# Where the two operands of a matmul lie, modulo 128 bytes, in a transformer block of fp32r matmuls

## The chip, the core and the metric

One core of a Trainium2 chip runs the whole kernel. The metric is the device time of one execution in microseconds; lower is better.

## What is computed

The reference is one transformer block on x of 32 x 256 x 256 with a context of 32 x 256 x 192: self attention, cross attention and a gated feed forward, each behind a layer norm and with a residual. There are 16 heads of 64, and the feed forward is 1024 wide.

```
def _attention(xq, xkv, wq, wk, wv, wo, bo):
    q = (xq @ wq).reshape(B, S, N_HEADS, D_HEAD)      # k, v alike from xkv
    attn = jnp.einsum('bihd,bjhd->bhij', q, k) * D_HEAD ** (-0.5)
    attn = jax.nn.softmax(attn, axis=-1)
    out = jnp.einsum('bhij,bjhd->bihd', attn, v).reshape(B, S, D_ATTN)
    return out @ wo + bo

h = _layernorm(x, ln1_g, ln1_b)
x = _attention(h, h, sa_wq, sa_wk, sa_wv, sa_wo, sa_bo) + x
h = _layernorm(x, ln2_g, ln2_b)
x = _attention(h, cond_emb, ca_wq, ca_wk, ca_wv, ca_wo, ca_bo) + x
h = _layernorm(x, ln3_g, ln3_b)
p = h @ ff_w1 + ff_b1
a, gate = (p[..., :D_FF], p[..., D_FF:])
return a * jax.nn.gelu(gate, approximate=False) @ ff_w2 + ff_b2 + x
```

## The kernel before

The kernel is written engine by engine: each engine has its own instruction list, and semaphores order them. Three stages follow each other: 32 passes of self attention, 32 of cross attention (64 passes in all, one batch each, software pipelined), and 32 iterations of the feed forward.

Every fp32 value that goes into a matmul is split into a high and a low part (`x_hi`, `x_lo`, both fp32r), and a product is the three matmuls high x high, high x low, low x high (`three` and `product`, L593). ACT writes the high part by a copy, DVE or POOL the low part by a subtraction. `nc.tensor.matmul(dst, a, b)` loads `a` into the array (a weight load, PEld) and streams `b` past it (PE). The profile's rows name the operands the other way round, streamed before loaded: `unit_ps<-w_hi,a_hi` streams `w_hi` and loads `a_hi`. One load and one matmul belong together, the load of the next runs beside the matmul before it.

A pass of attention has four steps. In each, PE does in order: `scores` of two head pairs (L606, 24 matmuls of 64 rows, in pairs for the left and the right half of the partitions), then the units of the step (`STEP_UNITS`: two q and k projections of 12 matmuls each, "v" of 6 with 512 columns, or "wo", the output projection of 24), then `attend` (L618, 16 matmuls). In the cross attention the output projection of the last step is cut in two, and its first 12 matmuls (`project_out(..., 0)`) stand straight behind the scores.

The feed forward runs over m = 0 to 7: `hidden(t, m)` is 12 matmuls into `s_ps` (value and gate), and `down(t, m - 2)` 6 matmuls into `unit_ps`, behind it. Between them ACT does the gelu and `a_hi`, DVE the gating, POOL `a_lo`. The first iteration (START) begins inside `end_attention`: PE does transposes, output half 0 of the last batch, attend, `hidden` of m = 0 to 2, attend, `hidden` of m = 3, output half 1, and then goes on with m = 4. The feed forward's three weights (two of `ff_w1` and `ff_w2`) are loaded into `w_stage` slots 0, 1 and 2 during the cross attention and split by `split_ff_weight` at the turn, while PE works.

| matmuls | loaded | streamed | before | changed |
|---|---|---|---|---|
| q and k projections, `hidden` | weights | `hT` | 0 / 64 | 0 / 64 |
| values ("v") | `hT` | weight | 64 / 0 | 64 / 0 |
| `scores` | queries | keys | 64 / 64 | 0 / 64 |
| `attend` | `v_f` | `pT` | 64 / 0 | 64 / 0 |
| output ("wo"), `down` | `a` | weight | 64 / 0 | 0 / 64 |

Of the kernel before, what the change touches and what calls it, by code (L numbers as in the profile page):

```python
# [10 lines left out]
P = 128  # L11
# [142 lines left out]
def columns_of(w, piece, slot):  # L154

    _, cols = columns(piece)
    if cols is None:
        return w[:, slot, piece[1] * DA:(piece[1] + 1) * DA]
    return w[:, slot, :].rearrange("p (k n) -> p k n", k=DK)[:, :, cols]

def block_kernel(nc, x, ctx, ln1_g, ln1_b, ln2_g, ln2_b, ln3_g, ln3_b, sa_wq, sa_wk, sa_wv, sa_wo, sa_bo,
# [4 lines left out]
    with stack:  # L167
# [50 lines left out]
        qk_hi = sb("qk_hi", [P, RING, 2, S], F32R)  # L218
        qk_lo = sb("qk_lo", [P, RING, 2, S], F32R)
# [213 lines left out]

        def tiles(a):
            return a.rearrange("(i p) d -> p i d", p=P)
# [12 lines left out]
        def _(sp):  # L448
# [15 lines left out]
            def load_cross_weight(slot, quarter):  # L464
# [4 lines left out]
                if w.shape[0] == DFF:  # L469
                    rows = PAIRS // 4  # L470
                    sp.dma_start(w_stage[:, slot, cols].rearrange("p (k n) -> p k n", k=rows),
# [3 lines left out]
                if w.shape[0] == DC and k:  # L475
                    sp.dma_start(w_stage[LEFT, slot, cols], w[P:, part]).then_inc(ca_ld, 16)
                    sp.dma_start(w_stage[RIGHT, slot, cols], w[P:, part]).then_inc(ca_ld, 16)
                else:
                    sp.dma_start(w_stage[:, slot, cols], w[k * P:(k + 1) * P, part]).then_inc(ca_ld, 16)

            def load_ff_weight(k, quarter):
# [3 lines left out]
                if len(w.shape) == 3:  # L485
                    rows = w.shape[1] // 4
                    sp.dma_start(w_stage[:, k, cols].rearrange("p (k n) -> p k n", k=rows),
                                 w[:, quarter * rows:(quarter + 1) * rows, :]).then_inc(ff_ld[k], 16)
                else:
                    sp.dma_start(w_stage[:, k, cols], w[:, cols]).then_inc(ff_ld[k], 16)  # L490
# [95 lines left out]
        def _(pe):  # L586
# [35 lines left out]
            def projection(slot, cols, side, tokens):  # L622

                terms = []
                for k in range(DK):
                    w = slice(k * DA + cols.start, k * DA + cols.stop)
                    if side == 1 and k == DK - 1:
                        terms += [(w_hi[:, slot, w], hT_hi[:, side, k, tokens]), (w_lo[:, slot, w], hT_hi[:, side, k, tokens])]
                    else:
                        terms += three(w_hi[:, slot, w], w_lo[:, slot, w], hT_hi[:, side, k, tokens], hT_lo[:, side, k, tokens])  # L630
                return terms

            def project_out(t, home, unit, it):
# [4 lines left out]
                if it == 0:  # L638
                    at.bank_free(pe, t, unit)
                    if isinstance(b, int) and b == ph.first:  # L640
# [5 lines left out]
                                for term in three(a_hi[:, m, rows], a_lo[:, m, rows], w_hi[:, 3, m * D:(m + 1) * D],  # L646
                                                  w_lo[:, 3, m * D:(m + 1) * D])])
# [696 lines left out]
```

## Time and profile before

| | |
|---|---|
| three runs, median | 2865.21 us (2864.95 to 2866.52) |
| the profiled execution: its time, its span | 2866.0 us, 2864.2 us |
| PE busy | 2842.0 us (99%), 25278 matmuls |
| DVE, ACT, POOL busy | 2256.3 (79%), 1912.3 (67%), 1471.1 us (51%) |
| granted clock of TensorE | 0.998 on average, 1.00 in the long stretches |

The profile is of one execution. Start times are records; the ends of matmuls are modelled and overlap, so how fast PE goes is read from the distance between starts or from a count of matmuls in a stretch, not from the mean duration of one. The self attention ends near 1180 us, the cross attention near 2306, the rest is the feed forward.

### The profile page before, as it was taken

Reading aid. Unit: us, or ns where it says so; the run is one execution under the profiler, and the core shown is the slowest. Engines: PE = TensorE matmul, PEld = TensorE weight load, DVE = VectorE, ACT = ScalarE, POOL = GpSimd, SP = SyncE. Lnnn points to the kernel's source line nnn. Section 1 sums busy time; section 2 is a strip of 40 time slices with the busy share of each in tenths; the row PEclk is TensorE's granted clock in tenths of the full one; section 3 lists DMA queues with packets and bytes.
Section 4 is the critical chain, followed back from the end, with each engine's and each line's share of the span. In section 5 each row is a group of like instructions: output and inputs, shape, how many; then the busy total and the mean of one; then the engine's idle time right before and its main releaser. Section 6 shows DMA issues by size and latency. Waiting matters only on the chain.

```text
span 2864.2 us, 72446 instructions
## 1 busy us (share of the span) xinstructions
PE 2842.0 (99%) x25278; PEld 2485.3 (87%) x25278; DVE 2256.3 (79%) x3495; ACT 1912.3 (67%) x6041; POOL 1471.1 (51%) x1310
## 2 busy tenths in 40 slices
PE   8999999999999999999999999999999999999999
PEld 6888888888888888888888888888888889999999
DVE  6888888888888888888888888888888865555554
ACT  6677766677766776777777777777777754444443
POOL 5444444444444444765555555555555544554554
PEclk9999999999999999999999999999999999999999
DMA  5666666666666666667777776666766632222222
GB/s 147 158 162 157 156 157 159 158 154 145 151 151 154 150 148 149 161 166 177 177 172 169 173 171 169 168 164 165 168 168 163 151 100 88 73 73 84 81 73 63
DMA packets 355360, 413.32 MB, mean 144 GB/s; under 512 B 122048, under 2 KB 209472, under 8 KB 355264
## 3 DMA queue, kind: packets, MB, share of 16 engines
q1 hardware_dynamic: 345120, 395.29, 57.4%
q10 hardware_dynamic: 10144, 16.78, 1.6%
q8 instruction: 56, 0.92, 0.1%
q14 instruction: 40, 0.33, 0.0%
HBM read 94.52 MB, written 49.02 MB: 50 GB/s over the span
## 4 chain that ended last, share of the span: by engine, by line
PE 98%; DVE 1%; ACT 1%; POOL 0%; issue 0%; DMA 0%; DVEq 0%; POOLq 0%; ACTq 0%
PE unit_ps L593 54%; PE o_ps L618 17%; PE s_ps L606 14%; PE s_ps L593 12%; DVE neg_max L1021 0%; ACT probs L851 0%; DVE blocks L1035 0%; POOL probs L1253 0%; DMA x_ln<-in_x_dram 0%; ACT qk_hi L882 0%; DVE qk_lo L1046 0%; DVE hT L1016 0%; DVE hT_lo L1059 0%; ACT x_n L828 0%; ACT L828 0%
## 5 line engine op out<-in xcount | busy, mean ns | idle before, releaser
L1253 POOL TENSOR_TENSOR probs<-probs,row_inv 128x1024 f32<-128x1024 f32 x512 | 967.8, 1896 | 893.9 <-DVE row_inv L1026 893.9
L851 ACT ACTIVATE probs<-s_ps,neg_max 128x256 f32<-128x256 f32 x2048 | 950.4, 487 | 403.9 <-DVE neg_max L1021 403.4
L1021 DVE TENSOR_REDUCE neg_max<-s_ps 128x4 f32<-128x1024 f32 x512 | 616.8, 1205 | 62.8 <-PE s_ps L606 58.4
L1035 DVE STREAM_TRANSPOSE blocks<-probs 128x1024 f32<-128x1024 f32 x512 | 633.2, 1237 | 19.9 <-POOL probs L1253 19.9
L593 PE MATMUL unit_ps<-hT_hi,w_hi 128*128 128x256 f32 x2048 | 571.3, 282 | 3.0 <-DVE hT_lo L1059 2.6
L593 PE MATMUL unit_ps<-hT_hi,w_lo 128*128 128x256 f32 x2048 | 554.0, 277 | 0.0
L618 PE MATMUL o_ps<-pT,v_f 128*64 128x256 f32 x4096 | 498.5, 385 | 1.7 <-DVE a_lo L1041 1.7
L593 PE MATMUL unit_ps<-hT_lo,w_hi 128*128 128x256 f32 x1792 | 496.1, 277 | 0.0
L851 ACT ACTIVATION_READ_ACCUMULATOR probs<-s_ps,neg_max 128x1 f32 x2048 | 444.6, 217 | 0.0
L593 PE MATMUL unit_ps<-w_hi,a_hi 128*128 128x256 f32 x1536 | 430.8, 280 | 3.8 <-DVE a_lo L1041 2.8
L593 PE MATMUL unit_ps<-w_lo,a_hi 128*128 128x256 f32 x1536 | 425.7, 277 | 0.0
L593 PE MATMUL unit_ps<-w_hi,a_lo 128*128 128x256 f32 x1536 | 425.7, 277 | 0.0
L618 PEld LDWEIGHTS o_ps<-pT,v_f 128*64 128x64 f32 x4096 | 271.7, 136 | 174.6 <-issue 48.0
L1046 DVE TENSOR_TENSOR qk_lo<-unit_ps,qk_hi 128x512 fp32r<-128x512 f32 x512 | 350.8, 685 | 76.8 <-ACT qk_hi L882 62.5
L593 PEld LDWEIGHTS unit_ps<-hT_hi,w_hi 128*128 128x128 f32 x2048 | 384.3, 188 | 21.2 <-issue 1.5
L593 PEld LDWEIGHTS unit_ps<-hT_hi,w_lo 128*128 128x128 f32 x2048 | 384.6, 188 | 0.0
L593 PEld LDWEIGHTS unit_ps<-hT_lo,w_hi 128*128 128x128 f32 x1792 | 336.8, 188 | 5.7
L1268 POOL TENSOR_TENSOR a_lo<-probs,a_hi 128x256 fp32r<-128x256 f32 x256 | 188.3, 741 | 264.9 <-ACT a_hi L900 263.0
L895 ACT ACTIVATE probs<-s_ps,b_col 128x256 f32<-128x256 f32 x256 | 121.7, 476 | 300.2 <-PE s_ps L593 300.2
L606 PE MATMUL s_ps<-qk_hi 64*128 64x256 f32 x2048 | 315.2, 304 | 6.0 <-DVE qk_lo L1046 6.0
L882 ACT CAST qk_hi<-unit_ps 128x512 fp32r<-128x512 f32 x512 | 313.9, 613 | 6.4 <-PE unit_ps L593 4.6
L1080 DVE SCALAR_TENSOR_TENSOR probs<-s_ps,b_col,probs 128x256 f32<-128x256 f32 x256 | 123.4, 482 | 240.7 <-ACT probs L895 238.7
(73 smaller groups left out, 6017.8 us busy)
## 6 DMA issues: line engine op xcount, KB each, us to landing
pT<-blocks SPq DMA_DIRECT2D x1024, 256.0 KB, 4.5
rows_t_dram<-row_blocks SPq DMA_DIRECT2D x91, 256.0 KB, 4.4
rows_in<-rows_t_dram SPq DMA_DIRECT2D x91, 256.0 KB, 4.1
x_res<-in_x_dram SPq DMA_DIRECT2D x32, 256.0 KB, 4.1
x_sa_dram<-x_out SPq DMA_DIRECT2D x32, 256.0 KB, 4.3
x_ln<-x_sa_dram ACTq DMA_DIRECT2D x32, 256.0 KB, 4.9
ctx_in<-in_ctx_dram SPq DMA_DIRECT2D x32, 256.0 KB, 4.4
x_res<-x_sa_dram SPq DMA_DIRECT2D x32, 256.0 KB, 4.1
```

What stands on the lines that cost most here:

```text
L593: last = nc.tensor.matmul(dst, a, b, start=start and n == 0, stop=stop and n == len(terms) - 1)
L606: last = nc.tensor.matmul(s_ps[:, m % 2, hd, it * S:(it + 1) * S], q[part, r, 0, rows], k[part, r, 1, :], start=n == 0, stop=n == 2)
L618: last = nc.tensor.matmul(o_ps[part, i, :], v_f[:, jt, 2 * (2 * n + i) + hd, :], p[:, jt, hd], start=jt == 0, stop=jt == IT - 1)
L851: op = nc.scalar.activation(probs[:, m % 2, r, :].rearrange("p (j b c) -> p j b c", j=IT, c=BLK), scored.rearrange("p (j c b) -> p j b c", ...
L882: nc.scalar.copy(qk_hi[:, unit[1] % RING, :, :], bank.rearrange("p (a s) -> p a s", a=2)).then_inc(at.qk_hi, 1)
L895: nc.scalar.activation(gate[:, m % 2, :], s_ps[:, m % 4 // 2, m % 2, S:2 * S], ACT.Gelu, bias=b1_col[:, FT + m:FT + m + 1]).then_inc(ff.ga ...
L1021: nc.vector.tensor_reduce(neg_max[:, m % RING, :], s_ps[:, m % 2, :, :].rearrange("p h (i j) -> p (h i) j", j=S), AX_X, ALU.max, negate=Tr ...
L1035: nc.vector.transpose(blocks[:, n % 2, :, m % 2, :].rearrange("p b (j r c) -> p r j b c", j=IT, c=BLK), probs[:, m % 2, :, :].rearrange("p ...
L1046: nc.vector.tensor_tensor(qk_lo[:, m % RING, :, :], unit_ps[:, bank_of(("qk", m)), :].rearrange("p (a s) -> p a s", a=2), f32(qk_hi[:, m % ...
L1080: nc.vector.scalar_tensor_tensor(hid[:, m % 2, :], s_ps[:, m % 4 // 2, m % 2, 0:S], b1_col[:, m:m + 1], gate[:, m % 2, :], ALU.add, ALU.mu ...
L1253: nc.gpsimd.tensor_tensor(probs[:, m % 2, :, :], probs[:, m % 2, :, :], row_inv[:, m % RING, :].unsqueeze(2).broadcast_to([P, ROWS, S]), A ...
L1268: nc.gpsimd.tensor_tensor(a_lo[:, m, :], hid[:, m % 2, :], f32(a_hi[:, m, :]), ALU.subtract).then_inc(ff.u_lo, 1)
```

## The change

The slots 0 to 2 of the weights now form `w_hi_loaded` and `w_lo_loaded`; slot 3, the one that is streamed by output and `down`, becomes a tensor of its own behind 16 floats, so at 64 modulo 128. `ff_w2` goes into slot 3 and no longer into slot 2. Since slot 3 holds the output weight until the last output projection, its split waits for that, half by half. The fillers around `a_hi` and `a_lo` are gone, which puts them at 0. Queries and keys of a head pair get a gap of 16 floats, so the keys lie 1088 bytes behind their queries and not 1024, and a filler ahead puts the queries at 0.

```
-        w_hi = sb("w_hi", [P, 4, WCOLS], F32R)
-        w_lo = sb("w_lo", [P, 4, WCOLS], F32R)
-        w_stage = sb("w_stage", [P, STAGES, WCOLS])
+        def weights(name):
+            loaded = sb(f"{name}_loaded", [P, 3, WCOLS], F32R)
+            sb(f"{name}_between", [P, 16])
+            streamed = sb(f"{name}_streamed", [P, WCOLS], F32R)
+            sb(f"{name}_behind", [P, 16])
+            return [loaded[:, i, :] for i in range(3)] + [streamed[:]]
+
+        w_hi, w_lo = weights("w_hi"), weights("w_lo")
+        w_raw = sb("w_raw", [P, STAGES, WCOLS])
+        w_stage = [w_raw[:, i, :] for i in range(STAGES)]
...
-        qk_hi = sb("qk_hi", [P, RING, 2, S], F32R)
-        qk_lo = sb("qk_lo", [P, RING, 2, S], F32R)
+        sb("before_queries", [P, 16])
+        qk_hi = sb("qk_hi", [P, RING, 2, S + 16], F32R)[:, :, :, 0:S]
+        qk_lo = sb("qk_lo", [P, RING, 2, S + 16], F32R)[:, :, :, 0:S]
+        sb("behind_queries", [P, 16])
...
-        sb("before_attended", [P, 16])
         a_hi = sb("a_hi", [P, PAIRS, S], F32R)
         a_lo = sb("a_lo", [P, PAIRS, S], F32R)
-        sb("behind_attended", [P, 16])
...
@@ down (PE)
                     last = product(bank[:, 0:D], three(a_hi[:, m, rows], a_lo[:, m, rows],
-                                                       w_hi[:, 2, m * D:(m + 1) * D], w_lo[:, 2, m * D:(m + 1) * D]),
+                                                       w_hi[3][:, m * D:(m + 1) * D], w_lo[3][:, m * D:(m + 1) * D]),
...
@@ iteration of the feed forward (PE)
                         for d in {4: (0,), 5: (1,), 6: (2, 3), 7: (4, 5)}.get(m, ()) if parts == START else ...
+                            if d == FT // 2 and parts == START:
+                                pe.wait_ge(ff_w2_lo, 2)
                             down(t, d)
...
@@ ACT
+            def split_down_weight(half):
+                act.wait_ge(at.wo_full, 2 * TOTAL - 1 + half)
+                if half == 0:
+                    act.wait_ge(ff_ld[2], 16 * 4)
+                cols = down_half(half)
+                nc.scalar.activation(w_hi[3][:, cols], w_stage[2][:, cols], ACT.Copy).then_inc(ff_hi_done, 1)
...
-                split_ff_weight(2)
+                split_down_weight(0)
...
@@ iteration of the feed forward (ACT; POOL has the same two lines, after its residual)
+                    if m == BEGUN and parts == START:
+                        split_down_weight(1)
...
@@ POOL
+            def split_down_weight(half):
+                pool.wait_ge(ff_hi_done, 3 + half)
+                cols = down_half(half)
+                nc.gpsimd.tensor_tensor(w_lo[3][:, cols], w_stage[2][:, cols], f32(w_hi[3][:, cols]), ALU.subtract).then_inc(ff_w2_lo, 1)
```

The order of PE's instructions stays as it was. In the last iterations of the feed forward, `down` between two `hidden` reads in the kernel before:

```order
L593 MATMUL s_ps<-hT_hi,w_lo 128x256
L593 MATMUL unit_ps<-w_hi,a_hi 128x256 [waits ff_u_lo]
L593 MATMUL unit_ps<-w_lo,a_hi 128x256
L593 MATMUL unit_ps<-w_hi,a_lo 128x256
L593 MATMUL unit_ps<-w_hi,a_hi 128x256
L593 MATMUL unit_ps<-w_lo,a_hi 128x256
L593 MATMUL unit_ps<-w_hi,a_lo 128x256
L593 MATMUL s_ps<-hT_hi,w_hi 128x256 [waits ff_hid_done]
```

and in the changed one:

```order
L603 MATMUL s_ps<-hT_hi,w_lo_loaded 128x256
L603 MATMUL unit_ps<-w_hi_streamed,a_hi 128x256 [waits ff_u_lo]
L603 MATMUL unit_ps<-w_lo_streamed,a_hi 128x256
L603 MATMUL unit_ps<-w_hi_streamed,a_lo 128x256
L603 MATMUL unit_ps<-w_hi_streamed,a_hi 128x256
L603 MATMUL unit_ps<-w_lo_streamed,a_hi 128x256
L603 MATMUL unit_ps<-w_hi_streamed,a_lo 128x256
L603 MATMUL s_ps<-hT_hi,w_hi_loaded 128x256 [waits ff_hid_done]
```

Only the tensors have changed. On ACT, at the turn from attention to feed forward, the kernel before has (the first row is the split of slot 1, `a_hi<-o_ps` are the evacuations of attend, `b_col` marks the gelu):

```order
L805 ACTIVATE w_hi<-w_stage 128x2048 [waits ff_ld1]
L904 CAST hT_hi<-hT 128x512 [waits ff_h_done,at_v_full]
L805 ACTIVATE w_hi<-w_stage 128x2048 [waits ff_ld2]
L861 CAST a_hi<-o_ps 128x512 [waits at_wo_full,at_o_full]
```

and the changed one, with the rows around m = 4 behind it:

```order
L817 ACTIVATE w_hi_loaded<-w_raw 128x2048 [waits ff_ld1]
L923 CAST hT_hi<-hT 128x512 [waits ff_h_done,at_v_full]
L824 ACTIVATE w_hi_streamed<-w_raw 128x1024 [waits ff_ld2,at_wo_full]
L880 CAST a_hi<-o_ps 128x512 [waits at_wo_full,at_o_full]
...
L919 CAST a_hi<-probs 128x256 [waits ff_hid_done]
L824 ACTIVATE w_hi_streamed<-w_raw 128x1024 [waits at_wo_full]
L914 ACTIVATE probs<-s_ps,b_col 128x256 [waits ff_hid_done,ff_p_full]
```

The split of the down weight has become two halves, each with a wait on an output projection. On POOL the same place in the changed kernel reads (before, the first row was one of 128x2048 and the second, `L1294`, was not there):

```order
L1294 TENSOR_TENSOR w_lo_streamed<-w_raw,w_hi_streamed 128x1024 [waits ff_hi_done]
L1289 TENSOR_TENSOR a_lo<-probs,a_hi 128x256 [waits ff_u_hi]
...
L1289 TENSOR_TENSOR a_lo<-probs,a_hi 128x256 [waits ff_u_hi] x3
L1261 TENSOR_TENSOR x_rb<-x_res,out_bias 128x512 [waits ff_res_ld]
L1294 TENSOR_TENSOR w_lo_streamed<-w_raw,w_hi_streamed 128x1024 [waits ff_hi_done]
L1289 TENSOR_TENSOR a_lo<-probs,a_hi 128x256 [waits ff_u_hi] x4
```

The second half stands behind the residual `x_rb` and ahead of the `a_lo` of m = 4.

## Rows read from the trace of the kernel before

**Rows 1.** The page, whole run: busy time of the engines; chain by engine.
```profile
PE 2842.0 (99%) x25278; PEld 2485.3 (87%) x25278; DVE 2256.3 (79%) x3495; ACT 1912.3 (67%) x6041; POOL 1471.1 (51%) x1310
...
PE 98%; DVE 1%; ACT 1%; POOL 0%; issue 0%; DMA 0%; DVEq 0%; POOLq 0%; ACTq 0%
```

**Rows 2.** Table by stretches: self attention and feed forward (columns: stretch, length, then by engine).
```profile
300.00:1150.00 850.00, 850.00 (x7599) 719.57 (x7600) 702.49 (x1019) 597.90 (x1968) 407.66 (x301) 1.00 0.65 153
...
2350.00:2850.00 500.00, 500.00 (x4309) 500.00 (x4308) 275.50 (x593) 206.50 (x510) 249.67 (x385) 1.00 0.26 77
```

**Rows 3.** Timeline (start us, us, engine, line): last key remainder, first load of scores.
```profile
1830.28 0.69 DVE L1046 TENSOR_TENSOR qk_lo<-unit_ps,qk_hi 128x512 fp32r<-128x512 f32 x1 [0.30 <-ACT qk_hi L882]
...
1831.18 0.19 PEld L606 LDWEIGHTS s_ps<-qk_hi 64*128 64x128 f32 x2 [0.38 <-DVE qk_lo L1046]
```

**Rows 4.** Timeline of PE, feed forward: starts of two successive m and a third.
```profile
2342.09 0.28 PE L593 MATMUL s_ps<-hT_hi,w_hi 128*128 128x256 f32 x1
...
2344.22 0.28 PE L593 MATMUL s_ps<-hT_hi,w_hi 128*128 128x256 f32 x1
...
2344.57 0.28 PE L593 MATMUL s_ps<-hT_hi,w_hi 128*128 128x256 f32 x1
...
2346.27 0.28 PE L593 MATMUL s_ps<-hT_hi,w_hi 128*128 128x256 f32 x1
```

**Rows 5.** Timeline of PE, self attention: projection behind scores, then output.
```profile
508.15 0.28 PE L593 MATMUL unit_ps<-hT_lo,w_hi 128*128 128x256 f32 x1
...
508.50 0.28 PE L593 MATMUL unit_ps<-hT_lo,w_hi 128*128 128x256 f32 x1
...
513.38 0.28 PE L593 MATMUL unit_ps<-w_hi,a_lo 128*128 128x256 f32 x1
```

**Rows 6.** Timeline of PE: two stretches of hidden, each behind an attend.
```profile
2319.66 0.28 PE L593 MATMUL s_ps<-hT_hi,w_hi 128*128 128x256 f32 x1
...
2323.29 0.28 PE L593 MATMUL s_ps<-hT_hi,w_lo 128*128 128x256 f32 x1
...
2325.60 0.28 PE L593 MATMUL s_ps<-hT_lo,w_hi 128*128 128x256 f32 x1
...
2326.77 0.28 PE L593 MATMUL s_ps<-hT_hi,w_lo 128*128 128x256 f32 x1
```

**Rows 7.** Timeline of PE, batch 29 of the feed forward: down of m = 2, then m = 3.
```profile
2813.75 0.28 PE L593 MATMUL unit_ps<-w_hi,a_hi 128*128 128x256 f32 x1
...
2814.45 0.28 PE L593 MATMUL s_ps<-hT_hi,w_hi 128*128 128x256 f32 x1
...
2816.51 0.28 PE L593 MATMUL s_ps<-hT_hi,w_hi 128*128 128x256 f32 x1
```

**Rows 8.** Timeline of PE, cross attention: output behind scores, then a projection.
```profile
1501.39 0.28 PE L593 MATMUL unit_ps<-w_lo,a_hi 128*128 128x256 f32 x1
...
1502.68 0.28 PE L593 MATMUL unit_ps<-hT_hi,w_hi 128*128 128x256 f32 x1
...
1503.04 0.28 PE L593 MATMUL unit_ps<-hT_hi,w_hi 128*128 128x256 f32 x1
```

**Rows 9.** Timeline of PE: pairs of score matmuls, the second and the last of twelve.
```profile
506.53 0.28 PE L606 MATMUL s_ps<-qk_lo,qk_hi 64*128 64x256 f32 x2
...
507.72 0.28 PE L606 MATMUL s_ps<-qk_hi,qk_lo 64*128 64x256 f32 x2
```

**Rows 10.** Groups by shape, whole run: busy us, mean ns of one.
```profile
L1268 POOL TENSOR_TENSOR a_lo<-probs,a_hi 128x256 fp32r<-128x256 f32 x256 | 188.3, 741 | 264.9 <-ACT a_hi L900 263.0
...
L1248 POOL TENSOR_TENSOR w_lo<-w_stage,w_hi 128x1024 fp32r<-128x1024 f32 x8 | 19.2, 2403 | 2.3 <-ACT w_hi L799 1.4 <-DVE hT_lo L1063 0.9
...
L799 ACT ACTIVATE w_hi<-w_stage 128x1024 fp32r<-128x1024 f32 x8 | 8.8, 1094 | 0.5 <-ACT x_n L828 0.5
```

**Rows 11.** Timeline at the start of the feed forward: residual; first matmul of down of m = 4.
```profile
2332.97 1.28 POOL L1240 TENSOR_TENSOR x_rb<-x_res,out_bias 128x512 f32<-128x512 f32 x1
...
2338.62 0.28 PE L593 MATMUL unit_ps<-w_hi,a_hi 128*128 128x256 f32 x1
```

More of the change, by code:

```diff
@@ L432, in straight, with down_half @@
             return rows.rearrange("p (k j c) -> p k j c", c=BLK, j=NB)
+        def down_half(half):
+            return slice(half * WCOLS // 2, (half + 1) * WCOLS // 2)
         def tiles(a):
@@ L470, in load_cross_weight @@
                     rows = PAIRS // 4
-                    sp.dma_start(w_stage[:, slot, cols].rearrange("p (k n) -> p k n", k=rows),
+                    sp.dma_start(w_stage[slot][:, cols].rearrange("p (k n) -> p k n", k=rows),
                                  w.rearrange("(k p) n -> p k n", p=P)[:, quarter * rows:(quarter + 1) * rows, :]).then_inc(ca_ld, 16)
@@ L475, in load_cross_weight @@
                 if w.shape[0] == DC and k:
[L476 to L477 removed]
+                    sp.dma_start(w_stage[slot][LEFT, cols], w[P:, part]).then_inc(ca_ld, 16)
+                    sp.dma_start(w_stage[slot][RIGHT, cols], w[P:, part]).then_inc(ca_ld, 16)
                 else:
[L479 removed]
+                    sp.dma_start(w_stage[slot][:, cols], w[k * P:(k + 1) * P, part]).then_inc(ca_ld, 16)
             def load_ff_weight(k, quarter):
@@ L486, in load_ff_weight @@
                     rows = w.shape[1] // 4
-                    sp.dma_start(w_stage[:, k, cols].rearrange("p (k n) -> p k n", k=rows),
+                    sp.dma_start(w_stage[k][:, cols].rearrange("p (k n) -> p k n", k=rows),
                                  w[:, quarter * rows:(quarter + 1) * rows, :]).then_inc(ff_ld[k], 16)
                 else:
-                    sp.dma_start(w_stage[:, k, cols], w[:, cols]).then_inc(ff_ld[k], 16)
+                    sp.dma_start(w_stage[k][:, cols], w[:, cols]).then_inc(ff_ld[k], 16)
             def in_register(value):
@@ L627, in projection @@
                     if side == 1 and k == DK - 1:
-                        terms += [(w_hi[:, slot, w], hT_hi[:, side, k, tokens]), (w_lo[:, slot, w], hT_hi[:, side, k, tokens])]
+                        terms += [(w_hi[slot][:, w], hT_hi[:, side, k, tokens]), (w_lo[slot][:, w], hT_hi[:, side, k, tokens])]
                     else:
-                        terms += three(w_hi[:, slot, w], w_lo[:, slot, w], hT_hi[:, side, k, tokens], hT_lo[:, side, k, tokens])
+                        terms += three(w_hi[slot][:, w], w_lo[slot][:, w], hT_hi[:, side, k, tokens], hT_lo[:, side, k, tokens])
                 return terms
@@ L645, in project_out @@
                                [term for m in range(half * HALF, (half + 1) * HALF)
-                                for term in three(a_hi[:, m, rows], a_lo[:, m, rows], w_hi[:, 3, m * D:(m + 1) * D],
-                                                  w_lo[:, 3, m * D:(m + 1) * D])])
+                                for term in three(a_hi[:, m, rows], a_lo[:, m, rows], w_hi[3][:, m * D:(m + 1) * D],
+                                                  w_lo[3][:, m * D:(m + 1) * D])])
                 if it == IT - 1:
@@ L694, in hidden @@
                     last = product(s_ps[:, m % 4 // 2, m % 2, half * S:(half + 1) * S],
-                                   [term for k in range(DK) for term in three(w_hi[:, k, cols], w_lo[:, k, cols],
+                                   [term for k in range(DK) for term in three(w_hi[k][:, cols], w_lo[k][:, cols],
                                                                               hT_hi[:, parity, k, :], hT_lo[:, parity, k, :])])
@@ L1299, in iteration @@
                         deviation(ff, t + 2)
+                    if m == BEGUN and parts == START:
+                        split_down_weight(1)
                     if "cur" in parts:
```

11 lines of the change are left out of this document (5 added, 6 removed).

## The prediction

> **What bounds the kernel now.** I read the page first, then the table by stretches, the chain of waits, and last the timeline of PE alone, because the first three say that only its finest grain is left. The page gives PE 99% of the span and the chain that ended last lies on PE for 98% of it [rows 1]. In the stretches by time PE has no idle time at the full granted clock of 1.00, while DVE is busy for 83% (702.49 of 850.00 us) and 55% (275.50 of 500.00), ACT and POOL for less [rows 2]. No other engine is close, and the one that feeds the scores is early: the key remainder is written at 1830.28 + 0.69 = 1830.97 and the scores' first weight load comes at 1831.18 [rows 3]. So the time is the sum over PE's matmuls of the distance from one start to the next; the ends in the profile are modelled, the starts are records. Only a change of that spacing, or of the stalls between kinds of work, moves the total.
>
> **Two spacings.** In the feed forward 4309 matmuls take 500 us, 116.0 ns each [rows 2]. The timeline shows that this is a mean of two values. One m (12 matmuls of `hidden`, 6 of `down`) goes from 2342.09 to 2344.22, 118.3 ns each, the next from 2344.22 to 2346.27, 113.9 ns [rows 4]; their mean, 116.1, is that of the 500 us, so they alternate through the whole feed forward. The instructions are the same in both. In the attention, 43 spacings of a projection and the output from 508.50 to 513.38 take 4.88 us, 113.5 ns each [rows 5]. I call 113.4 (the 32 spacings of [rows 6] in 3.63 us) the short spacing and 118 the long one.
>
> What decides between them? Sorted by the places of the two operands, the rows say this. (a) `hidden` and the q, k projections have the loaded operand at 0 and the streamed one at 64; `down` and the output have 64 and 0. (b) A `down` at the short spacing is followed by a `hidden` at the long one, which keeps it and hands it to its `down`; the next `hidden` needs 0.35 us for three spacings and is short from then on [rows 4]. (c) It is not m's parity. The long m that starts at 2342.09 is m = 1, all odd ones are like it, and in batch 29, m = 2 starts short, but its `down` takes 0.70 us for six, 117 ns, from 2813.75 to 2814.45, after a single matmul that came a few ns late. The next m, 3, is then short, 2.06 us to 2816.51 [rows 7], and odd and even have changed places up to the end. So the spacing is a state that the stream carries along, and the change of kind at the end of `down` switches it. (d) An output block straight behind scores (in the cross attention) runs at the long spacing, 1501.39 to 1502.68 for 11 spacings, and the projection behind it needs 0.36 us for three and then is short [rows 8]. A projection straight behind scores needs 0.35 us for its first three spacings, 508.15 to 508.50, and is short from there [rows 5]. (e) Scores, 64 against 64, have ten spacings of pairs in 1.19 us, 119 ns [rows 9].
>
> **The change, term by term.** It puts all of output, `down`, `hidden`, projections and scores at loaded 0 and streamed 64. Values (loaded 64, streamed 0) and attend stay.
>
> 1. Feed forward. The switch between kinds at the end of each `down` is gone. If the stream stays at 113.4, it gains 116.0 - 113.4 = 2.6 ns on each of 4608 matmuls (32 batches x 8 m x 18, by the code): 12.2 us. Bounds: nothing (116.0 stays), and all at 118, which costs (118 - 116.0) x 4608 = +9.2 us. I take the gain, because (a) to (d) put the loss at the switch and a uniform stretch of both kinds has held the short spacing for 43 in a row.
> 2. Scores. 64 x 4 steps x 10 spacings = 2560. The trace has no scores at 0 and 64. The nearest rows are single matmuls at those places, 113.4, and today's 119. I take 117, since a pair is two loads and two matmuls and each start has its own spacing in the unit, and since the first three after a start are longer anywhere: -2.0 x 2560 = -5.1 us. Bounds: 113.4 gives -14.3; the long spacing carried over (119 + 2.7) gives +6.9 us.
> 3. Output behind scores, in 32 passes of the cross attention: 11 x (117.3 - 113.4) + 3 x (120 - 116) = 55 ns each, -1.7 us; bounds 0 and -2.0.
> 4. The turn. The down weight now lies where the output weight lay, so its split into high and low part waits for the output projection, in two halves. One copy of 128x2048 on ACT becomes two of 128x1024 (1.09 us each), one subtraction on POOL becomes two of 2.40 us [rows 10]. The first half waits on ACT for output half 0 of the last batch; behind it on ACT stands only the evacuation of the attend that PE begins after that output and that takes longer than 1.09 us (16 matmuls, 8 pairs of over 0.2 us). The second stands on ACT before the gelu of m = 4 and is released when the output ends. PE then still has the 12 matmuls of `hidden` of m = 4 before it, 1.4 us, so the copy of 1.09 us is hidden with 0.3 us to spare. On POOL it stands behind the residual that ends at 2332.97 + 1.28 = 2334.25 and delays `a_lo` of m = 4 to 2336.65 + 0.74 = 2337.4 (0.74 is the 741 ns of one in [rows 10]); PE wants it, and the weight of the new wait, at 2338.62 [rows 11]. That is 1.2 us to spare, and `gated` of m = 6 on DVE, which waits for the same `a_lo`, has its gelu behind it and not PE. I put this at nothing; without that cover it would be 1 to 2 us, once.
> 5. A gap of 64 bytes between queries and keys makes the writes of `qk_hi` and `qk_lo` two runs of 256 instead of one of 512. The trace has no such pair of shapes to compare; the same elements are moved, so I take nothing, and even a tenth of 0.69 us would leave 0.14 of the 0.21 us before the scores' load [rows 3].
>
> The sum is -12.2 - 5.1 - 1.7 = -19.0 us. The profiled execution took 2866.0 us (its span 2864.2), which makes 2847.0; the median of the three runs, 2865.21, is 0.8 below it, so the sum gives 2846.2 there. I say 2847.0.
>
> **A rule against the change.** The stretches of [rows 4] are equal instructions at 118.3 and 113.9 ns, so loading and streaming do disturb each other here. The Trainium skill, TensorE: Matmul & The Clock Gate, "Step-by-step: what each phase is for", says otherwise: TensorE has two independent read ports, and loading the next weights takes no bandwidth from the running matmul. SBUF — State Buffer, "Who interferes with whom", adds that PE never waits on anyone. By that rule the places of the operands are nothing and terms 1 to 3 are zero; by the rows they are -19.0.
>
> **The rivals.**
> - *Places don't matter (the loss hangs on something else that alternates, such as the destination bank).* For it: the forecast rests on correlation in one trace. Against: (c), since the banks kept their order when the spacings changed places. Time 2865.2. Chance 0.06.
> - *The long spacing is kept.* This one ends on the other side. In a uniform stream nothing switches, so nothing lifts the stream out either. For it: a `hidden` that starts behind attend, already at 0 and 64, takes 1.17 us for the ten spacings from 2325.60 to 2326.77, 117 ns, and does not recover [rows 6], and every recovery of the feed forward is at a switch. Against: the other start of that kind is short from its fourth matmul, as are all behind scores and values. If the feed forward sits at 118, the terms give +9.2 - 5.1 - 1.7 = +2.4 us, 2867.6 (chance 0.09); if the scores keep it too, +9.2 + 6.9 - 1.7 = +14.4, 2879.6 (chance 0.04). It decides from the point where 57% of the feed forward's matmuls are long (2.6 / 4.6), where term 1 is zero.
> - *Scores alone get slower*, the loads of two halves meeting the streams in a worse way: -12.2 - 1.7 + 6.9 = -7.0, 2858.2. Chance 0.12.
> - *The feed forward gains only in part*, long after each start or small delay until something lifts it: half of term 1, 2852. Chance 0.04.
> - The forecast: 0.65. Its own range is 2842 to 2853.
>
> **How the numbers follow.** The lower end, 2838, takes nearly the whole bound of term 2 (2865.2 - 12.2 - 14.3 - 1.7 = 2837.0). The upper end, 2861, takes in scores that get slower and the partial gain; left out are the first two rivals, 0.19. The three runs of before lie within 1.6 us, and 0.2% (5.7 us) is about what a measurement can tell from no change. Faster than 2859.5: forecast, scores alone, part of the gain, 0.81, less 0.02 for the edges of those ranges; slower than 2870.9: 0.04 and a share of the milder case of the second rival, 0.07; the rest, 0.14, is within.
>
> **What the profile of the changed kernel would show.** Term 1: 18 matmuls of each m in 2.04 us, no alternation, and 4410 matmuls in 500 us. Term 2: ten spacings of score pairs in 1.17 us. Term 3: the output block behind scores at 113 to 114 ns. Term 4: no idle time of PE between 2320 and 2345. The forecast is wrong if the feed forward still has two spacings, or one at 118, or if the scores' pairs stand at 120 and more.

## The result: 2875.5 us, slower by 0.31%

The changed kernel takes 2875.53 us (median of 8 runs, 2873.01 to 2876.85), the kernel before beside it 2866.31 us (8 runs). The ratio is 1.0031, 95% interval 1.0020 to 1.0042. The prediction said 2847.0 us, and its range ended at 2861.

The page of the changed kernel (busy time, then the chain that ended last) answers to [rows 1]:

```profile
PE 2851.5 (99%) x25278; PEld 2491.1 (87%) x25278; DVE 2258.2 (79%) x3495; ACT 1909.2 (66%) x6042; POOL 1469.6 (51%) x1311
...
PE 98%; DVE 1%; ACT 0%; POOL 0%; issue 0%; DMA 0%; DVEq 0%; POOLq 0%; ACTq 0%
```

PE is still the bound, with as many matmuls, and is busy 9.5 us longer. The table by stretches answers to [rows 2]:

```profile
300.00:1150.00 850.00, 850.00 (x7543) 718.74 (x7542) 698.19 (x1013) 592.77 (x1954) 403.54 (x299) 1.00 0.65 152
2350.00:2850.00 500.00, 500.00 (x4356) 500.00 (x4355) 279.97 (x604) 207.74 (x514) 254.51 (x393) 1.00 0.26 78
```

In 850 us of self attention PE now starts 7543 matmuls and not 7599; in 500 us of feed forward 4356 and not 4309, 114.8 ns each and not 116.0. So the feed forward gained and the attention lost. Measured from the first score matmul of a pass to that of the next, in the timeline of PE:

- a pass of self attention 36.97 us, before 36.71: +0.267 x 31 = +8.3 us;
- a pass of cross attention 35.07 us, before 34.91: +0.160 x 31 = +5.0 us;
- an m of the feed forward 2.067 us, before 2.127 and 2.053 in turn, mean 2.090: -0.023 x 248 = -5.7 us;
- the turn: from the last score matmul to the end it is 558.7 us, before 560.4; with the feed forward's -5.7 taken out, +3.9 us.

The last score matmul starts 12.4 us later than before (the two lines on the passes give 13.3, since the first and last pass of each kind are incomplete). 12.4 - 5.7 + 3.9 = +10.6; the spans, 2874.9 and 2864.2, differ by 10.7.

**Feed forward.** Timeline of PE, starts of `hidden`, `down` and the next `hidden`:

```profile
2601.94 0.28 PE L603 MATMUL s_ps<-hT_hi,w_hi_loaded 128*128 128x256 f32 x1
...
2603.30 0.28 PE L603 MATMUL unit_ps<-w_hi_streamed,a_hi 128*128 128x256 f32 x1
...
2604.00 0.28 PE L603 MATMUL s_ps<-hT_hi,w_hi_loaded 128*128 128x256 f32 x1
```

Twelve matmuls of `hidden` take 1.36 us, 113.3 ns each, in nearly every m (241 of 253): the alternation of [rows 4] is gone. But six of `down` take 0.70 us, 117 ns. **Output** in self attention, from its first matmul to the attend behind it:

```profile
402.23 0.28 PE L603 MATMUL unit_ps<-w_hi_streamed,a_hi 128*128 128x256 f32 x1
...
405.14 0.44 PE L628 MATMUL o_ps<-pT,v_f 128*64 128x256 f32 x2
```

It takes 2.91 us for 24; the block of before took 2.81, at the short spacing of [rows 5]. That is 91 ns, twice a pass, 5.6 us over 31 passes. Both are the kinds that the change moved from 64/0 to 0/64 modulo 128.

**The turn.** The waits of PE between 2300 and 2345 us (engine, line, waited for: us in total, times, longest), then the timeline there:

```profile
PE s_ps L603 <- DVE hT_lo L1115: 3.2, 1, 3.2
```

```profile
2330.53 2.90 DVE L1115 TENSOR_TENSOR hT_lo<-hT,hT_hi 128x512 fp32r<-128x512 f32 x1
...
2330.16 2.72 POOL L1294 TENSOR_TENSOR w_lo_streamed<-w_raw,w_hi_streamed 128x1024 fp32r<-128x1024 f32 x1 [5.47 <-ACT w_hi_streamed L824]
```

The first `hidden` waits 3.2 us for `hT_lo`, which takes 2.90 us and ends 0.55 us behind POOL's half of the down weight's subtraction. The profile of before has no wait for `hT_lo` there.

### The profile page after: what moved, and what is told of

It reads as the page before. It is cut to its first block, busy times and chain, and to the rows that moved or that the text cites. A ratio compares the mean times of both kernels' runs of the same rounds, so it can differ in the third digit from the quotient of the medians.

```text
span 2874.9 us, 72450 instructions
## 1 busy us (share of the span) xinstructions
PE 2851.5 (99%) x25278; PEld 2491.1 (87%) x25278; DVE 2258.2 (79%) x3495; ACT 1909.2 (66%) x6042; POOL 1469.6 (51%) x1311
## 4 chain that ended last, share of the span: by engine, by line
PE 98%; DVE 1%; ACT 0%; POOL 0%; issue 0%; DMA 0%; DVEq 0%; POOLq 0%; ACTq 0%
PE unit_ps L603 55%; PE o_ps L628 16%; PE s_ps L616 14%; PE s_ps L603 12%; DVE neg_max L1042 0%; DVE blocks L1056 0%; ACT probs L870 0%; POOL probs L1274 0%; DMA x_ln<-in_x_dram 0%; ACT qk_hi L901 0%; DVE w_lo_loaded L1008 0%; PE unit_ps L768 0%; DVE hT_lo L1115 0%; DVE qk_lo L1067 0%; DVE hT L1037 0%
## 5 line engine op out<-in xcount | busy, mean ns | idle before, releaser
L603 PE MATMUL unit_ps<-hT_hi,w_hi_loaded 128*128 128x256 f32 x2048 | 572.7, 283 | 1.9 <-DVE hT_lo L1080 1.5
L603 PE MATMUL unit_ps<-hT_hi,w_lo_loaded 128*128 128x256 f32 x2048 | 556.2, 278 | 0.0
L603 PE MATMUL unit_ps<-hT_lo,w_hi_loaded 128*128 128x256 f32 x1792 | 497.3, 278 | 0.0
L603 PE MATMUL unit_ps<-w_hi_streamed,a_hi 128*128 128x256 f32 x1536 | 433.4, 282 | 3.8 <-DVE a_lo L1062 2.8
L603 PE MATMUL unit_ps<-w_hi_streamed,a_lo 128*128 128x256 f32 x1536 | 429.8, 280 | 0.0
L603 PE MATMUL unit_ps<-w_lo_streamed,a_hi 128*128 128x256 f32 x1536 | 429.8, 280 | 0.0
L603 PEld LDWEIGHTS unit_ps<-hT_hi,w_hi_loaded 128*128 128x128 f32 x2048 | 384.8, 188 | 20.9 <-issue 1.6
L603 PEld LDWEIGHTS unit_ps<-hT_hi,w_lo_loaded 128*128 128x128 f32 x2048 | 384.9, 188 | 0.0
L603 PEld LDWEIGHTS unit_ps<-hT_lo,w_hi_loaded 128*128 128x128 f32 x1792 | 337.5, 188 | 6.0
```

The lines of the kernel that those rows point to most:

```text
L603: last = nc.tensor.matmul(dst, a, b, start=start and n == 0, stop=stop and n == len(terms) - 1)
```

## The experiments

Five kernels named micro leave the whole block out and run only TensorE's stream. The others compute everything. The excerpts of code are shortened to the lines that matter. A place is a byte address modulo 256, of which 0, 64, 128 and 192 occur. The kernel before has the weights at 128 and `hT`, `a`, queries and keys at 64. In the changed kernel the loaded weights lie at 128 (high part) and 0 (low part), the streamed ones at 192 and 64, `a` at 128, queries and keys at 128 and 192 or at 0 and 64 by slot. The text on the change speaks only of modulo 128. `v_f` and `pT` also move by 128 in the changed kernel; micro3 has a configuration with these two moved alone, and its passes stay within 2 ns, so they are left aside.

**micro1: a map of places**

```python
for s in range(PLACES):
    for l in range(PLACES):
        apart()                       # one matmul on 64 rows
        for i in range(24):
            matmul(ps[:, 0, 0:256], at(loaded, l, i % 2, 128), at(streamed, s, i % 2, 256))
```

> A kernel with nothing but matmuls; the whole block is left out. For each of 16 places of the loaded and 16 of the streamed operand, 64 bytes apart and taken modulo 1024, it issues 24 matmuls of 256 columns with all 128 rows, then pairs on two halves of 64 rows, then for 4 by 4 places matmuls of 512 columns. Theory A (the prediction's): what counts is the place modulo 128, so the 16 by 16 table of the mean spacing is a checkerboard of four kinds that repeats every two places, with 113.4 ns at loaded 0 and streamed 64 and about 118 at others. Theory B: a larger period counts, 256 or more, so that the output of the changed kernel (loaded 128, streamed 64 or 192 modulo 256) reads 118 in the table and the kernel before (loaded 64, streamed 128) reads 113.4. Theory C: places count for nothing, and all 256 cells are within 1 ns of one another.

The mean of the last 12 spacings in each stretch, worked out from the starts, repeats every 256 bytes and in nothing smaller (one cell takes either 118.4 or 120.0):

```
ns per matmul      loaded 0   64     128    192
streamed   0       120.0     113.3   118.4  117.8
          64       113.3     120.0   117.8  118.8
         128       118-120   117.8   120.0  113.3
         192       113.3     119.0   113.3  120.0
```

The rows of the timeline show it without any working. They are the single matmuls ahead of (loaded 0, streamed 64), ahead of (64, 64) and behind that:

```profile
71.78 0.32 PE L51 MATMUL ps<-streamed,loaded 64*128 64x128 f32 x1
...
74.95 0.32 PE L51 MATMUL ps<-streamed,loaded 64*128 64x128 f32 x1
...
78.26 0.32 PE L51 MATMUL ps<-streamed,loaded 64*128 64x128 f32 x1
```

3.17 us for the one and 3.31 for the other, with the same instructions. Theory A falls: loaded 0 and streamed 64 modulo 128 is four cells of this table, three at 113.3 and one, (128, 64), at 117.8, and that one is the low weight's place under output and `down` of the change. Pairs of matmuls on 64 rows, in the mean of the ten spacings behind the first, do best, 57.0 to 57.5 ns per matmul, where the loaded operand is 64 bytes behind the streamed one modulo 256; at 64 and 64, as before, they take 59.0 to 59.6, and 64 bytes ahead, as in the change, 58.9 or 59.0.

**micro2: the kernel's own order, TensorE alone**

```python
for c in CONFIGS:                     # places of weights, hT, a, queries, keys
    for unit in "SvpvOSpwOSvpvOSpwO" + "hd" * 9:
        part(c, unit)                 # scores, values, projections, attend, output, hidden, down
```

> TensorE's stream of the kernel by itself (one self-attention pass and nine m of the feed forward, in the kernel's order, with its hi and lo terms), for many places of the operands in SBUF; no other engine works and the rest of the block is left out. Theory B (places modulo 256 bytes decide, the table of micro1): with the places of the kernel before, one pass takes about as long per block as in its profile and the m of the feed forward take 2.05 to 2.13 us; with those of the change the output blocks take about 90 ns more and each m about 2.07 us, though no other engine works; and with weights at 0, hT at 64 and a at 64 modulo 256 each m takes 18 x 113.3 = 2.04 us and an output block of 24 takes 2.72 to 2.80 us. Theory D (other engines' traffic in SBUF disturbs the loads): the differences between the places of before and of the change are gone when TensorE is alone.

With the places of before, m takes 2.127 and 2.053 us in turn, as in the kernel; with those of the change 2.067, and its output block 2.905. No other engine runs, so theory D falls for these two: the places of TensorE's own operands are enough. Two forecasts were wrong. With weights at 0, `hT` and `a` at 64, m takes 2.072 and 2.108 us and the output block 2.823. And the self-attention pass hardly differed, 36.89 us with the places of before and 36.88 with those of the change, where the profiles have 36.71 and 36.97; micro4 finds why.

**w0, gap, turn: one piece at a time**

```diff
 w0:    +        sb("before_weights", [P, 32])
          w_hi = sb("w_hi", [P, 4, WCOLS], F32R)
          w_lo = sb("w_lo", [P, 4, WCOLS], F32R)
        +        sb("behind_weights", [P, 32])
 gap:   +        sb("before_queries", [P, 16])
        +        qk_hi = sb("qk_hi", [P, RING, 2, S + 16], F32R)[:, :, :, 0:S]      (qk_lo too)
 turn:  down reads slot 3; split_ff_weight(2) becomes split_down_weight(0) and (1), as in the change
```

> The kernel before with one edit: the weights begin 128 bytes later, at 0 modulo 256 in place of 128; everything else keeps its place modulo 256 bytes, and nothing changes its place modulo 128. Theory A (places modulo 128, the prediction's): no change, ratio 1.000. Theory B (places modulo 256, micro1): hidden and projections (loaded 0, streamed 64) and down and output (loaded 64, streamed 0) stand at 113.3 ns from a cold start, so each m of the feed forward takes 2.04 us and not 2.05 and 2.13 in turn: 12 us less, 1 to 2 us less from output behind scores, and 0 to 4 us more from values, where micro1 has 232.7 ns for 64 and 0 and 229.8 for 64 and 128: 2852 to 2857 us, ratio 0.995 to 0.997. Theory C (only the state of the stream counts): feed forward alternates as before.

2896.51 us, ratio 1.0113 (1.0096 to 1.0130). Nothing was moved modulo 128, so places modulo 128 can't be the rule. My own forecast from micro1 had the wrong sign. The timeline shows a projection behind scores, first matmul to the first of the output behind it:

```profile
399.54 0.39 PE L595 MATMUL unit_ps<-hT_hi,w_hi 128*128 128x256 f32 x1
...
402.48 0.28 PE L595 MATMUL unit_ps<-w_hi,a_hi 128*128 128x256 f32 x1
```

2.94 us, with 118 ns from start to end, at places (loaded 0, streamed 64) that micro1 ran at 113.3. The same places can hold either spacing; which one depends on how the stretch begins, here behind scores. The kernel before shows the same from the other side: the projection of [rows 5] loads at 128 and streams at 64, 117.8 in the map, and runs at the short spacing. micro2 has 2.936 us for this block in its place in the order, and 2.072 and 2.108 us for m; w0 has 2.931 and the same 2.072 and 2.108. A self pass is 0.453 us longer and a cross pass 0.533, the feed forward the same in the mean: 31 x 0.986 = +30.6 us. So the map of places is not enough; places and order together told this block and m.

> The kernel before with the queries and keys part of the change alone: queries at 128 or 0 modulo 256 and keys 1088 bytes behind. The prediction's term 2 gives -5.1 us. micro1's pairs give 58.9 ns per matmul for these places and 59.4 for those of before, so theory B expects 6144 x 0.5 = -3 us, less what the first projections behind scores lose (about 0.07 us a pass in the changed kernel, if the scores' places are its cause: +4). So between -3 and +1 us by theory B, with the scores' own ten spacings at 118.

2874.11 us, ratio 1.0031 (1.0018 to 1.0043): the scores' part of the change costs as much alone as the whole change, and my range of -3 to +1 us was wrong. The scores themselves gain, about 45 ns a pass of self attention and 22 of cross attention. What stands behind them loses in the cross attention: a projection behind scores 2.698 us and not 2.612, the output behind it 2.922 and not 2.814, though their own places are those of before: what the scores leave behind decides. A cross pass is 0.33 us longer, a self pass 0.08 shorter, in sum 7.6 us.

> The kernel before with the turn of the change alone: the down weight in slot 3, split behind the output projection in two halves, every place modulo 256 as before. The prediction's term 4: nothing. Rival (shared SBUF port of VectorE and GpSimd): GpSimd's first half, 2.4 to 2.7 us, starts before VectorE's hT_lo of the first feed forward batch and holds it from 0.69 to about 2.9 us; TensorE waits about 3 us there, and the total is 3 us longer, ratio 1.001.

2866.23 us, ratio 1.0003 (0.9993 to 1.0013). The turn alone costs nothing in the median, and in the profiled execution the collision doesn't happen. (The ten times reach from 2863.84 to 2869.35 us, three of them above 2868; whether it happens in those is not shown.) Timeline:

```profile
2318.30 0.69 DVE L1108 TENSOR_TENSOR hT_lo<-hT,hT_hi 128x512 fp32r<-128x512 f32 x1
...
2318.85 2.39 POOL L1287 TENSOR_TENSOR w_lo<-w_stage,w_hi 128x1024 fp32r<-128x1024 f32 x1 [6.39 <-ACT w_hi L817]
```

Here DVE comes first, by 0.55 us. In the changed kernel POOL came first, by 0.37. The clock differs between the two. The output whose end releases the first half runs at the granted clock of 0.50, 1.2 GHz, in this kernel (and in the one before), after a wait of 2.8 us for `a_lo`; in the changed kernel, after an equal wait, it runs at 1.00. The table by stretches, for turn and then for the changed kernel (the third number from the end is the granted clock):

```profile
2313.30:2315.80 2.50, 2.50 (x12) 2.50 (x13) 2.50 (x3) 0.76 (x1) 0.00 (x0) 0.50 1.06 265
```

```profile
2325.50:2328.40 2.90, 2.90 (x24) 2.82 (x24) 2.90 (x4) 0.80 (x1) 0.00 (x0) 1.00 1.03 251
2333.60:2336.60 3.00, 3.00 (x17) 3.00 (x18) 1.69 (x4) 0.71 (x1) 0.00 (x0) 0.63 0.00 0
```

So in the changed kernel the output ends 1.4 us earlier against DVE's work, POOL's half starts 0.9 us earlier, and the slow clock comes after the new wait instead. Why the clock fell at another point after the same wait is not settled. The new turn is not what keeps it up: gap, keys_first and best have the turn of before, their clock stayed at 1.00 there, and then PE waits for `hT_lo` in them too, 1.0 us. Waits of PE in gap between 2290 and 2355 us:

```profile
PE s_ps L595 <- DVE hT_lo L1096: 1.0, 1, 1.0
```

So about 2.2 of the 3.2 us belong to the longer `hT_lo`, the rest to an execution at full clock.

**turn_apart: the changed kernel without the collision**

```diff
                 residual(at, TOTAL - 1, ca.norm)
+                pool.wait_ge(ff.x_lo, 1)
                 split_down_weight(0)
```

> The changed kernel with one wait more: GpSimd's first half of the down weight's subtraction starts only when VectorE has written the first feed forward batch's hT_lo. Theory (the two shared a port): hT_lo takes 0.69 us and not 2.90, TensorE waits about 1 us and not 3.2 us between the last attend but one and the feed forward, and the total is 2 to 3.3 us less than the changed kernel's 2875.5, so about 2872.7, ratio to before 1.0025. Rival (hT_lo was long for another reason, or the wait only moves): 2875.5 as before it, ratio 1.003.

2872.06 us, ratio to before 1.0024 (1.0013 to 1.0035); its span, 2871.2, is 3.7 below that of the changed kernel, and the passes are the same. Of the 3.7, 2.2 are the shorter wait and most of the rest the slow clock behind it, which this execution doesn't have. Against the kernel before beside each, the medians differ by 7.0 us here and by 9.2 in the changed kernel; the two intervals of the ratio overlap. `hT_lo` is back at 0.68 us and the wait at 1.0:

```profile
2330.56 0.68 DVE L1115 TENSOR_TENSOR hT_lo<-hT,hT_hi 128x512 fp32r<-128x512 f32 x1
```

The collision is shown: the same instruction takes 2.90 us beside POOL's and 0.68 without it. The Trainium skill, SBUF — State Buffer, "Who interferes with whom", has it as a rule: a VectorE instruction with two SBUF inputs contends with a GpSimd instruction that reads SBUF. By that rule the trace agrees (0.68 and 2.90 us). The prediction never looked for it.

**micro3, micro4, micro5: how far the stream alone tells the time**

```diff
 micro3: high and low parts at places of their own; the cross-attention pass added
 micro4: slots of queries and keys 2048 bytes apart (micro2, micro3: shifted by 128 in every second slot)
 micro5: the places of change and after256, then 120 placements
```

> TensorE's stream alone again (a self-attention half pass twice, a cross-attention pass, six m of the feed forward), with high and low parts at places of their own and queries and keys apart from each other; the rest of the block is left out. Theory E (phase: the places modulo 256 bytes and the phase in which a stretch begins decide together, as micro2 suggests, since w0 and micro2 agree): with the places of each kernel already timed, the stream alone takes the time of its profile within 20 ns a pass: self-attention pass 36.71 us for before, 36.97 for the change, 36.63 for the gap alone; cross-attention pass 34.91, 35.07 and 35.23; m 2.127 and 2.053, 2.067, 2.127 and 2.053. Rival (other engines' accesses take part): the sums differ from these profiles by more than 0.1 us a pass. The sweep of the other places says whether some placement lies below all of them: theory E allows one, with no forecast of where.

For the change 36.972 and 35.091 us, for the gap alone 36.626 and 35.229, as expected, with 24 ns too much in one pass. For before 36.893 and 35.028, and the profile has 36.707 and 34.907. That looked like the rival, until I saw that my stream shifted every second slot of the queries by 128 bytes, which before doesn't.

> The stream alone, with the slots of queries and keys 2048 bytes apart, as in the kernel before (micro2 and micro3 had shifted every second slot by 128 bytes, as the change does). Theory E, the stream alone decides: with the places of the kernel before, the self-attention pass is now 36.71 us and the cross-attention pass 34.91, as in its profile (micro3, with the shift: 36.89 and 35.03). Rival: the 0.19 and 0.12 us between micro3 and the profile come from what other engines do, and stay. The second half gives six m of the feed forward for 256 placements of the four parts of down's operands, twice; theory E gives no forecast of the best, only that 18 x 113.3 = 2.04 us is the floor.

With the slots right, the stream alone gives 36.708 and 34.906 us for the places of before. Its timeline, first score matmuls of a half pass, of the cross pass and of what follows:

```profile
123.45 0.39 PE L82 MATMUL s_ps<-qk_hi 64*128 64x256 f32 x2
...
141.81 0.38 PE L82 MATMUL s_ps<-qk_hi 64*128 64x256 f32 x2
...
176.71 0.39 PE L82 MATMUL s_ps<-qk_hi 64*128 64x256 f32 x2
```

18.36 us is half of the 36.71, and 34.90 the cross pass. The second half found seven placements of `down` with 2.040 us for each m, all with the streamed weight at 64. The plainest has `a` at 0. First `hidden` of three m:

```profile
2480.56 0.28 PE L64 MATMUL s_ps<-hT_hi,w_hi 128*128 128x256 f32 x1
...
2482.60 0.28 PE L64 MATMUL s_ps<-hT_hi,w_hi 128*128 128x256 f32 x1
...
2484.64 0.28 PE L64 MATMUL s_ps<-hT_hi,w_hi 128*128 128x256 f32 x1
```

> The stream alone: a self-attention pass, a cross-attention pass and four m of the feed forward, first for the places of the changed kernel and of after256, then for 120 placements with queries and keys at one place or 64 bytes apart, with the weights of output and down at 128 (as before) or at 64 modulo 256 with a at 0. Theory E: the first configuration repeats the changed kernel's profile (36.97, 35.07 and 2.067 us) and the following ones tell after256 in advance; the m of the feed forward is 2.04 us wherever down's operands are at loaded 0 and streamed 64 modulo 256 and hidden's at 128 and 64. Rival: a pass or an m is off by more than 0.05 us.

The change's configuration gives 36.974 and 35.091 us, that of after256 36.626 and 35.100. Of its four m the two in the middle, which the ends of the short stretch don't touch, take 2.067 us for the change and 2.040 for after256 and for every placement with `down` at 0 and 64. No other placement beats keys_first in the attention.

**keys_first, after256, best: kernels chosen by the stream alone**

```diff
 keys_first (on before):
-        qk_hi = sb("qk_hi", [P, RING, 2, S], F32R)
+        sb("before_keys", [P, 32])
+        qk_hi = sb("qk_hi", [P, RING, 2, S + 16], F32R)[:, :, :, 0:S]      (qk_lo too)
-        q[part, r, 0, rows], k[part, r, 1, :]
+        q[part, r, 1, rows], k[part, r, 0, :]
 after256 (on the change):
-            sb(f"{name}_between", [P, 16])
+            sb(f"{name}_between", [P, 48])
-        sb("behind_queries", [P, 16])
+        sb("behind_queries", [P, 48])
 ...
 best (on keys_first):
+            raw = sb(name, [P, 4 * WCOLS + 48], F32R)
+            return [raw[:, i * WCOLS:(i + 1) * WCOLS] for i in (0, 1, 3, 2)], raw[:, 3 * WCOLS + 48:4 * WCOLS + 48]
```

> The kernel before with the keys ahead of the queries: loaded queries 64 bytes behind the streamed keys modulo 256 (keys at 192 and 64, queries at 0 and 128), nothing else moved modulo 256. By the prediction's rule of places modulo 128 this is the same kind as the change's scores (0 and 64), so theory A expects what the gap alone gave, 2874. Theory E reads micro3: self-attention pass 36.61 us and cross-attention pass 34.83, against 36.71 and 34.91 before, so 31 x 0.094 + 31 x 0.080 = 5.4 us less: 2860 us, ratio 0.998. The rival that this falls: the stream falls into its slower branch by other engines' timing, and the total is 2865 or more.

2860.21 us, ratio 0.9981 (0.9972 to 0.9990), forecast 2860. (The projections also write the other half of the bank, so that one copy still moves both.) Modulo 128 its scores are the change's, loaded at 0 and streamed at 64; modulo 256 the loaded one is 64 bytes behind and not ahead. A self pass is 36.613 us and a cross pass 34.827, within 1 ns what the stream alone had.

> The changed kernel with the same 0 and 64 of output and down, made to hold modulo 256 and not only modulo 128: a at 0 (not 128), the streamed weights, high and low, both at 64 (not 192 and 64), the loaded ones both at 128. Nine small tensors share one so that it fits. Theory A (places modulo 128): nothing changes, 2875.5. Theory E: micro4 gives 2.040 us for each m in place of 2.067, 6.6 us less; the output blocks go from 2.905 us to between 2.81 and 2.92, 0 to 11 us less; so 2857 to 2869.

2860.34 us, ratio 0.9981 (0.9971 to 0.9990): the changed kernel with output and `down` held to loaded 0, streamed 64 modulo 256, 15 us faster than the change. m takes 2.040 us, and the output in self attention 2.812. The 3.1 us wait at the turn is still in it. This kernel also moves the low part of the loaded weights back, from 0 to 128, so the 15 us are not those of output and `down` alone. micro5's third configuration is the change with only their places moved: 36.814 and 34.846 us a pass, m 2.040. Against the change in the same stream that is 31 x 0.160 + 31 x 0.245 + 248 x 0.027 = 19 us, an estimate for a kernel that was not run; the low part's return gains 0.19 us more in a self pass and loses 0.25 in a cross pass.

> The kernel before with keys_first's scores and, in the feed forward alone, down's operands at loaded 0 and streamed 64 modulo 256 (its weight 192 bytes behind the values' weight, which now lies in the last slot, and a written 64 bytes lower there); output, projections and values stay where they were. Theory E adds what was read apart: 5.4 us less from the two attention passes (micro5: 36.612 and 34.827 us, against 36.708 and 34.906) and 248 x (2.090 - 2.040) = 12.4 us less from the feed forward: 2865.2 - 17.8 = 2847.4, ratio 0.9938. Rival: the two don't add, since the feed forward keeps the phase in which the attention leaves it, as the kernel before does: 2860, ratio 0.998.

2847.70 us (5 runs, 2846.39 to 2849.05), ratio 0.9943 (0.9929 to 0.9956), forecast 2847.4. The two parts add. Its feed forward in 490 us (4223 matmuls in the kernel before, in the same 490):

```profile
2350.00:2840.00 490.00, 490.00 (x4323) 489.90 (x4321) 272.67 (x587) 206.18 (x511) 247.85 (x383) 1.00 0.26 78
```

## Why the prediction was wrong

**The step that failed** is (a) in "Two spacings": "`hidden` and the q, k projections have the loaded operand at 0 and the streamed one at 64; `down` and the output have 64 and 0", with places taken modulo 128. The trace of before cannot tell 0 from 128. Of the pairs that the change made under output and `down`, 128 with 192 occurs in no row of it, and 128 with 64 occurs only as that of `hidden` and the projections, which [rows 4] show at both spacings. Shown by w0 (nothing moves modulo 128, +31 us), by micro1's table, and by after256, which makes the same kind hold modulo 256 and gains 15 us, with micro5's third configuration.

**Term 1** (-12.2) was half right. That a uniform feed forward stays at 113.3 holds for `hidden`, and where the places suit, for all 18: 2.040 us in after256 and best, the forecast's number. In the change `down` stays at 117 to 118, and the term is -5.7. It lay within the term's own bounds.

**What had no term** was the rest of the attention. The prediction moved output and priced only its blocks straight behind scores; values and projections it took as unmoved, but modulo 256 their low weight goes from 128 to 0. A self pass is longer by 182 ns in output (91, twice), 72 in values and 53 in projections, and 39 shorter in scores; a cross pass by 131, 3 and 97 (75 in the projection behind output), and 69 shorter in scores. This is +12.4 us net up to the last scores, where terms 2 and 3 had -6.8. This is the larger part of the miss.

**Term 2** (-5.1) had the sign and two thirds of the size for the scores' own blocks, which in the change are 39 ns shorter in a self pass and 69 in a cross pass, -3.3 us; ten spacings of pairs take 1.16 to 1.18 us, forecast 1.17, and took 1.18 to 1.20 before. But they also decide how what follows runs, which gap shows to cost more than they gain. **Term 3** (-1.7) is nothing: 1518 ns and not 1520 for the block behind scores.

**Term 4**, the turn at nothing: the waits that it worked through were right (turn alone, 1.0003), but it asked only who waits for whom, not which engines run side by side. In the changed kernel POOL's first half starts 0.37 us ahead of `hT_lo` and stretches it from 0.69 to 2.90, which costs PE 2.2 us; the 3.7 by which turn_apart's span is shorter hold the slow clock as well, which not every execution has. Of the first half the term had said only that nothing but an evacuation stands behind it on ACT, and it had worked out spare time for the second half alone.

**Term 5**, the writes over the gap at nothing, was right: the median of `qk_lo` is 691 ns, before 692.

**The rivals.** That places don't matter, and with it the rule of the Trainium skill, TensorE: Matmul & The Clock Gate, "Step-by-step: what each phase is for", that loading the next weights takes no bandwidth from the running matmul, does not hold for these fp32r matmuls: 113.3 and 120.0 ns in micro1 differ by the addresses alone. "The long spacing is kept" came nearest, but for `down` and output, not for `hidden`. The claim (b) to (d), that the spacing is a state carried along, is borne out: gap changes the spacing of projections and output whose own places it leaves alone.

What stays open is why. The runs show a period of 256 bytes and two spacings for one pair of places, picked by what ran before; they don't show what in the memory makes them, and the map isn't symmetric (loaded 0, streamed 192 has 113.3, loaded 192, streamed 0 has 117.8).

## What to carry to other kernels

A correlation in one trace fixes a rule only over the places that this trace has: before an address is moved, write out where each operand lies by the largest power of two that might matter, and see whether the new pair occurs anywhere. A stream of one engine that is the bound can be run alone, in its own order and with its own addresses: here it gave each pass to 25 ns and, once it had the slots right, the time of keys_first and best to 1 us, where a table of isolated pairs had the wrong sign for w0. And when work is moved to another engine's idle time, look at what runs beside it, not only at what waits for it.

## What the runs showed of the hardware

- A full 256-column fp32r matmul starts every 113.3 ns or every 117.8 to 120.0, by the addresses of the loaded and the streamed operand modulo 256 bytes (micro1), with no other engine at work.
- The same addresses can hold either spacing for a whole block: (loaded 0, streamed 64) runs at 113.3 behind a single matmul in micro1 and at 118 behind scores in w0.
- Pairs of matmuls on 64 rows take 57.0 to 57.5 ns per matmul where the loaded operand lies 64 bytes behind the streamed one modulo 256, and 59.0 to 59.6 where both are at 64 (micro1).
- A VectorE subtraction with both inputs in SBUF took 2.90 us beside a GpSimd subtraction that had started 0.37 us before it, and 0.68 in the same kernel when the GpSimd one waited (turn_apart).
